# Writing the column of ones once for a ring of gather buffers, or once per gather

## The reference

```python
deg = segment_sum(jnp.ones(idx.shape[0], dtype=jnp.float32), idx, num_segments=n)
proj = jnp.einsum('ni,rio->rno', feat, W)      # 16 edge types r
m = proj[etypes, src_idx] + bias
m = m * norm_per_edge[:, None]                 # 1 / degree of the receiving node
return segment_sum(m, dst_idx, num_segments=n)
```

## Time and profile before

| | |
|---|---|
| median of 3 runs | 2248.73 us (2247.24 to 2249.34) |
| profiled execution | 2245.63 us |
| its span | 2243.7 us |
| TensorE busy | 2015.8 us, 90% |
| VectorE busy | 1138.3 us, 51% |
| GpSimd busy | 1027.6 us, 46% |
| mean granted TensorE clock | 0.960 of full speed |

### The profile page before, as it was taken

One profiled execution on the slowest core, in us unless ns is written; L12 is line 12 of the kernel. 1 busy time (PEld: TensorE's weight loads), 2 busy tenths in 40 slices (PEclk: granted clock), 3 DMA queues, 4 the chain that ended last, 5 costly groups with the idle time before them and its releaser, 6 DMA issues.

```text
span 2243.7 us, 26429 instructions
## 1 busy us (share of the span) xinstructions
PE 2015.8 (90%) x8235; PEld 1379.3 (61%) x8235; DVE 1138.3 (51%) x2452; ACT 605.0 (27%) x1262; POOL 1027.6 (46%) x1014
## 2 busy tenths in 40 slices
PE   7999999889999999898878788898989669999997
PEld 3456544355555555454545555677777668888897
DVE  4999950256666564433566656544455841111121
ACT  2333333211221221111422221222222552222242
POOL 0000000366666666666566666666665113333332
PEclk9999999999999999999899999999999579999999
DMA  7432335455555555556644444332334384444473
GB/s 276 158 136 95 134 155 229 159 158 177 179 178 179 178 168 182 178 181 165 184 144 138 146 138 122 90 90 87 87 90 80 128 288 112 125 116 120 128 194 67
DMA packets 136486, 333.20 MB, mean 149 GB/s; under 512 B 25344, under 2 KB 65952, under 8 KB 135072
## 3 DMA queue, kind: packets, MB, share of 16 engines
q1 hardware_dynamic: 80064, 199.64, 24.5%
q0 software_dynamic: 52992, 130.09, 23.1%
q10 hardware_dynamic: 3296, 1.80, 0.3%
HBM read 202.71 MB, written 128.71 MB: 148 GB/s over the span
## 4 chain that ended last, share of the span: by engine, by line
PE 80%; issue 6%; another core or an unknown queue 5%; DVE 4%; ACT 3%; DMA 2%; DVEq 0%; POOL 0%; SPq 0%; ACTq 0%; POOLq 0%
PE bank L679 29%; PE bank L748 15%; PE bank L1947 9%; PE bank L1958 8%; PE bank L1867 4%; PE bank L1876 4%; PE bank L586 3%; DVE arena L773 1%; PE bank L1777 1%; PE bank L1805 1%; DMA table_fwd<-arena 1%; PE bank L1765 1%; PE bank L1844 1%; PE bank L1916 1%
## 5 line engine op out<-in xcount | busy, mean ns | idle before, releaser
L679 PE MATMUL bank<-arena,work 128*128 128x512 f32 x1600 | 741.9, 600 | 14.2 <-ACT arena L672 9.0
L773 DVE TENSOR_TENSOR arena<-arena,bank 128x257 f32 x880 | 370.8, 421 | 529.7 <-PE bank L748 284.1
L748 PE MATMUL bank<-arena 128*128 128x257 f32 x1760 | 499.2, 396 | 71.1 <-DVE arena L773 37.6
L725 POOL DMA_INDIRECT arena<-table_bwd,arena x440 | 428.3, 974 | 237.4 <-issue 99.0
L725 POOL DMA_INDIRECT arena<-table_fwd,arena x440 | 437.2, 994 | 212.8 <-issue 99.8
L679 PEld LDWEIGHTS bank<-arena,work 128*128 128x128 f32 x1600 | 301.3, 192 | 296.5 <-issue 270.8
L672 ACT ACTIVATE arena<-bank 128x512 f32<-128x512 f32 x400 | 238.5, 598 | 777.4 <-PE bank L679 551.7
L748 PEld LDWEIGHTS bank<-arena 128*128 128x128 f32 x1760 | 327.7, 197 | 194.8 <-issue 153.7
L1017 POOL DMA_INDIRECT out<-xn,work x56 | 89.4, 1597 | 250.9 <-DVE xn L192 181.3
L1947 PE MATMUL bank<-xn,arena 128*128 128x256 f32 (+1 forms) x1120 | 203.0, 340 | 0.0
L734 DVE TENSOR_TENSOR arena<-cst,arena 128x512 f32<-128x512 f32 x220 | 151.2, 689 | 102.0 <-PE bank L679 102.0
(11 more groups left out here) (315 smaller groups left out, 1563.8 us busy)
## 6 DMA issues: line engine op xcount, KB each, us to landing
table_fwd<-arena SPq DMA_DIRECT2D x100, 512.0 KB
table_bwd<-arena SPq DMA_DIRECT2D x100, 512.0 KB
arena<-in_W SPq DMA_DIRECT2D x35, 1024.0 KB
arena<-in_W SPq DMA_DIRECT2D x2, 4096.0 KB, 14.3
arena<-table_fwd,arena POOLq DMA_INDIRECT x440
arena<-table_bwd,arena POOLq DMA_INDIRECT x440
work<-x_transposed SPq DMA_DIRECT2D x50, 128.0 KB
mix_rows<-arena SPq DMA_DIRECT2D x25, 256.0 KB
```

Source lines behind the costliest of these rows:

```text
L679: last = pe.matmul(ps[4 + s % 2][:, :], xT[t % 2][:, k * P:(k + 1) * P], ar(W_off[d] + k * 4096 + c * 512, 512), start=(k == 0), stop=(k = ...
L725: e.indirect_dma_start(msg[b][:, 0:C], None, table[d], bass.IndirectOffsetOnAxis(ap=idx[d][:, n % TE:n % TE + 1], axis=0)).then_inc(s_ga[b ...
L748: pe.matmul(ps[sum_bank(n)][:, 0:W], oh[b], msg[b], start=True, stop=True).then_inc(s_sm, 1)
L773: vec.tensor_tensor(to, to, ps[sum_bank(n)][:, 0:W], ALU.add).then_inc(s_ac, 1)
```

## The change

GpSimd no longer writes the ones once. `gather` writes the one column of its ring place (128x1) right ahead of the gather into it, and each MEMSET raises the counter `ones_set`. `sum_tile` waits for that counter to reach n + 1; before, TensorE waited once, for 1, ahead of all sums.

```diff
-        msg_ones = ar(R2, RING * W).rearrange("p (j w) -> p j w", w=W)[:, :, C]
...
             d, b = n // TE, n % RING
             G.wait(s_sm, n - RING + 1)
+            nc.gpsimd.memset(msg[b][:, C:W], 1.0).then_inc(s_ones, 1)
             e.indirect_dma_start(msg[b][:, 0:C], None, table[d], bass.IndirectOffsetOnAxis(
                 ap=idx[d][:, n % TE:n % TE + 1], axis=0)).then_inc(s_ga[b], 16)
...
             b = n % RING
+            e.wait_ge(s_ones, n + 1)
             e.wait_ge(s_ga[b], 16 * (n // RING + 1))
...
                 e.wait_ge(s_pj, SLOTS)
-                nc.gpsimd.memset(msg_ones, 1.0).then_inc(s_ones, 1)
                 e.wait_ge(s_post, 1)
...
                 e.wait_ge(s_gmr, 2)
-                e.wait_ge(s_ones, 1)
                 e.wait_ge(s_xT, NT)
```

## The result

The changed kernel takes 2260.47 us (median of 4 runs, 2254.43 to 2262.86) beside 2247.98 us for the kernel before (4 runs, 2245.89 to 2249.34): ratio 1.0046, interval 1.0029 to 1.0064 (the ratios here are not the quotients of the two medians; they can differ from them by 0.1%). It is slower by some 7 to 14 us by that interval, 12.5 us between the medians, where the forecast was no change. Its profiled execution took 2254.43 us, with a span of 2252.7 us, 9.0 us more than the span in the earlier trace rows.

A forecast was written before the change was run, and what follows sets the result against it. TensorE was taken as the bound, with 80% of the chain. New GpSimd work hidden under ring waits and TensorE's waits counted 0, the start +0.3 us: 2249.0 us as median, no change; range 2243 to 2268 us.

The forecast's parts named there:

- The removed MEMSET: GpSimd before the tables land: dropping the one 16-column MEMSET, 0.127 us long, is worth 0.
- The price of a MEMSET: GpSimd's queue ahead of each gather: a 128x1 MEMSET costs 0.10 us, bounds 0.03 to 0.43, 44 us a stage.
- fixed step: GpSimd, between gathers: 0.30 us of idle time stands before every gather, making 1.25 us from start to start.
- Hidden under the waiting for ring places: Both gather stages: 44 us of new GpSimd work each is covered by 76.4 and 97.1 us of waiting.
- The first rival: Both gather stages: GpSimd becomes the bound from c = 0.174 us; 2268 us at c = 0.25, 2427 at 0.43; chance 0.16.
- The moved wait: GpSimd: waiting for a free ring place moves from the gather to the MEMSET ahead of it, costing 0.
- +0.3 us at the start: First gathers after the tables: the first MEMSET adds 0.1 us to the path; +0.3 us is counted in all.
- The lead: Ring of 16 places: a gather starts 23.5 us ahead of its sum, with some 19 us to spare.
- TensorE's 221 wait instructions: TensorE's queue at the sums: 221 more wait instructions, 9 to 13 us as the upper end, taken as 0.
- the second rival: TensorE's queue pays for the added wait instructions: 13 us, 2262 us; chance 0.06.
- The sum: Whole kernel: only +0.3 us is added, giving 2249.0 us as median, no change.
- The last gather still near 1731 us: End of the backward gathers: a sign that the forecast is right, the last gather not moving from about 1731 us.

The follow-up runs named there:

- two MEMSETs: Kernel before plus two 128x1 MEMSETs into spare columns ahead of each gather: 2079.45 us beside 2079.18, ratio 0.9999.
- with waits: Kernel before plus 864 never-blocking GpSimd wait instructions ahead of gathers, no write: 2079.78 us beside 2079.18 (0.9998); 2265.41 beside 2229.95 (1.0153).
- four MEMSETs: Kernel before plus four 128x1 MEMSETs into spare columns ahead of each gather: 2253.68 us beside 2229.95, ratio 1.0102.
- the four experiments of that chip: Kernel before with GpSimd's MEMSETs alone 1.0020, with TensorE's waits alone 0.9999; changed kernel with a sum's waits swapped 1.0024, ones awaited once per four sums 1.0026.
- the spare MEMSET: Kernel before plus one 128x1 MEMSET into spare columns ahead of each gather: 2252.5 us beside 2247.47 (1.0020); 2238.83 beside 2229.95 (1.0038).

## Why the prediction was right or wrong, step by step

The measured 2260.47 us lies inside the stated range, 2243 to 2268, but that is luck. The forecast itself was no change, within 0.2%, and 0.46% came. The range reached so far up only for the sake of GpSimd as the bound (2268), and the nearest single number was that of TensorE's wait instructions (2262); the runs refute both.

**The removed MEMSET.** Worth 0: no run speaks against it.

**The price of a MEMSET, c = 0.10 us, bounds 0.03 to 0.43.** Too dear, and the lower bound too high. On the fast chip, where hardly any waiting covers it, it is under 2 ns: the MEMSET runs inside the 0.30 us that stands before every gather anyway. The prediction had this idle time as a fixed step and did not ask what of it could be filled. The lower bound was the 0.03 us from one MEMSET to the next where they follow each other; of one, two and four per gather, four are the first to show something, 0.05 us in all. The Trainium skill's rule cited in the prediction (GPSIMD Engine Reference, Instruction dispatch), that an instruction's completion doesn't hold back the next one on the engine, gave the nearer of the two prices, 0.03 us; the rows with two MEMSETs, 0.12 us long and 0.03 us apart, agree with it.

**Hidden under the waiting for ring places, 0.174 and 0.221 us a gather.** The waiting was there, but it did not shrink as foretold. The 101.9 us named after L749, where 160.5 were, look like it and are a matter of naming: a wait of a gather includes the fixed 0.30 us, and a wait of the MEMSET ahead of it doesn't (160.5 - 207 x 0.30 = 98.4). Between gathers, beyond 0.30 us each (and without the step between the stages), GpSimd waits 174.1 us before and, with the MEMSETs counted as part of the 0.30, 174.4 us now. So the 44 us a stage were not covered by this waiting; they never came. The first rival (GpSimd becomes the bound from c = 0.174) is refuted by its price.

**The moved wait: 0, and +0.3 us at the start.** The first gather came 0.39 us later and not 0.1: the first step behind the tables is 0.10 of MEMSET and 0.70 of idle time where the earlier trace rows has 0.84 us of idle time alone, and the release itself also came later (420.19 for 419.82 us), which I can't put down to the change. A small term either way. The lead was somewhat less than the 16 x 1.468 = 23.5 us of the prediction, 20.1 us from a gather's start to its sum in the median of the trace of before, which changes nothing here.

**TensorE's 221 wait instructions: 0.** Right: 0.9999, and the second rival (2262 us) falls with it, though its number lies nearest to the result.

**The sum.** This is the step that failed: that the new 44 us a stage are "covered by that waiting" was taken as the whole bill for GpSimd's side, so that what fits under the waiting costs nothing. On the fast chip it holds (0.9996). On the first and the third it does not: 0.2 to 0.5% is lost by GpSimd's added instructions although each is hidden, the ring is still waited for as long as before, and past the first 50 every gather starts at least 13 us ahead of its sum. What the runs show in the place of "covered" is idle time of TensorE's: 12.3 us more of it from the first gather to the last. "The last gather still near 1731 us" failed with it: 1742.2. The profile of before had a sign of such a chip, 78.2 us of GpSimd's waits and 5% of the chain without a named releaser; I read them as more waiting for sums, that is as cover. They do wait for sums; what I didn't ask is why the trace can't name the sum.

**What stays open.** How a hidden instruction of GpSimd costs time on these two chips. What the runs bound: it comes from GpSimd's side, it needs no write and no raised counter, it isn't the gathers' pace, it grows from one MEMSET to four and is greatest with waits, and it is absent on a chip whose engines never start late behind TensorE.

Two accounts are nearest. One is that a ring place is reused later, since GpSimd reacts later to a sum: from a sum's end to the gather that it releases the least time in the records is 0.27 us before, 0.31 in the changed kernel, 0.41 with four MEMSETs and 0.75 with waits (worked out from the traces of single executions), in the order of the losses. Against it, gathers still start some 20 us ahead of their sums, and past the first 50 never less than 13 us, so a few tenths should cost nothing.

The other is that more instructions which touch counters make TensorE's late steps more or longer. Single traces don't show it for the MEMSETs (840 us before and 861 in the changed kernel, 823 to 862 in the four experiments of that chip; on the third chip 819 in the changed kernel, 901 with the spare MEMSET, 857 with four), and hint at it at most for the waits (941). The kernel with the MEMSET behind the gather would have told them apart: there the least time from a sum to its gather is back at 0.27 us. But it ran only on the fast chip, where nothing is to be told.

A third, that the longer program is slower to load, has little for it: the instruction queues (q8 and q14 of the page) move 134 packets before, 142 in the changed kernel, 141 with the waits and 162 with four MEMSETs, 0.3% of the DMA time in each, and 143 in the changed kernel on the fast chip. No account is shown. No version here beats the kernel before: on the first and third chips it leads, on the fast one all are alike.

## What to carry to other kernels

Before pricing a small instruction by its record, look for a fixed gap between the records of its engine: what fits in the gap has no price even where the engine is the bound. "Hidden" is still no promise of zero: on two chips whose profiles have waits with no named releaser, 880 added instructions on an engine that works 13 us or more ahead of the bound cost 0.2 to 0.5%. A total of waits named after one engine can shrink because a fixed gap is no longer counted in it: compare whole idle times before calling a cover used up. And a difference of a few tenths of a per cent should be timed on more than one chip, each against its own run of the kernel before.

## What the runs showed of the hardware

- The same kernel takes 2079, 2230 and 2247 us on three chips. The first 420 us are alike in the two traces compared (the changed kernel's); 169.2 of the 175.3 us between their spans lie between the first gather and the last.
- On the slower ones, in those stages, engines begin some of their work up to several us after the product that they wait for: 447 steps of TensorE's counters come over 0.5 us late in the kernel before, 840 us in sum; none on the fast chip.
- On the fast chip, where the gathers set the pace, a 128x1 MEMSET ahead of each costs under 2 ns, and two cost the same. The step from gather to gather is 1.25 us with none and about the same with one or two; with four (third chip) it is 1.30 us.
- 864 wait instructions on GpSimd that never block cost nothing on the fast chip (0.9998) and 1.5% on the third (1.0153). One MEMSET a gather costs 0.4% there (1.0038) and four 1.0% (1.0102).
